# Routed experts: the activations are transposed between the next block's up products, and split first thing in a tick

## The reference

```python
# layer 0
topv, topi = jax.lax.top_k(logits, TOP_K)
gate = jax.nn.softmax(topv, -1)
weights = jnp.zeros_like(logits).at[bidx, sidx, topi].set(gate)
a = jax.nn.silu(jnp.einsum('bsd,edh->bseh', h, w1)) * jnp.einsum('bsd,edh->bseh', h, w3)
y = jnp.einsum('bseh,ehd->bsed', a, w2)
moe = jnp.einsum('bsed,bse->bsd', y, weights)
return x + moe
# layer 1
gate_up = jnp.einsum('th,eoh->teo', xf, w1)
act = _silu_and_mul(gate_up)
moe_out = jnp.einsum('te,tei,ehi->th', combine, act, w2)
return (moe_out + shared_out).reshape(B, S, Hd)
```

## Time and profile before

| | us |
|---|---|
| median of 3 runs | 2915.37 |
| lowest, highest | 2915.37, 2922.96 |
| the profiled execution | 2915.24 |
| its span (first to last instruction) | 2913.6 |
| routed experts of layer 0, in the span | about 1238 to 1605.6 |
| routed experts of layer 1, in the span | about 2486 to 2913.6 |

### The profile page before, as it was taken

How to read it: one execution, slowest core, us unless ns; L and a number is a source line. 1 busy time by engine, 2 the same in 40 slices (tenths; PEclk the granted TensorE clock), 3 DMA queues, 4 the chain that set the end, 5 groups by cost and what they waited for, 6 DMA issues and landing times. The chain is left out here.

```text
span 2913.6 us, 50292 instructions
## 1 busy us (share of the span) xinstructions
PE 2610.7 (90%) x15547; PEld 2140.7 (73%) x15548; DVE 1720.7 (59%) x3323; ACT 1130.1 (39%) x2430; POOL 782.3 (27%) x792
## 2 busy tenths in 40 slices
PE   7889879979789989879997798998999999699997
PEld 6778757768578877668875477676777788688886
DVE  4525857659676757566664447774444426566664
ACT  1102336633143324445543123564544432344442
POOL 3202200004232324423232200660000012355554
PEclk9999889999889989989998699999999989899998
DMA  4434122214532134377774432445122030666663
GB/s 158 158 115 120 26 81 71 68 38 147 145 113 61 33 121 128 117 218 226 197 215 91 119 95 47 138 135 156 56 75 71 21 114 11 189 157 159 158 159 65
DMA packets 289046, 332.99 MB, mean 114 GB/s; under 512 B 147206, under 2 KB 202454, under 8 KB 287073
## 3 DMA queue, kind: packets, MB, share of 16 engines
q1 hardware_dynamic: 216640, 250.73, 27.6%
q0 software_dynamic: 20640, 51.74, 9.2%
q10 hardware_dynamic: 51584, 28.17, 3.4%
HBM read 233.86 MB, written 96.72 MB: 113 GB/s over the span
## 5 line engine op out<-in xcount | busy, mean ns | idle before, releaser
L840 PE MATMUL e_psum<-e_up_hi,hT_hi 128*128 x672 | 245.7, 366 | 23.1 <-DVE hT_lo L810 14.6
L841 PE MATMUL e_psum<-e_up_lo,hT_hi 128*128 x672 | 237.6, 354 | 0.0
L842 PE MATMUL e_psum<-e_up_hi,hT_lo 128*128 x672 | 237.5, 353 | 0.0
L840 PEld LDWEIGHTS e_psum<-e_up_hi,hT_hi 128*128 128x128 f32 x672 | 127.4, 190 | 46.0 <-issue 33.3
L1421 POOL TENSOR_TENSOR self_a_p<-self_a_p,self_a_mx 112x448 f32<-112x448 f32 x96 | 96.6, 1007 | 228.3 <-DVE self_a_mx L1478 228.3
L816 DVE TENSOR_TENSOR hT_lo<-e_psum,hT_hi 128x256 fp32r<-128x256 f32 (+2 forms) x138 | 55.7, 435 | 154.9 <-ACT hT_hi L756 147.9
L738 ACT ACTIVATE e_gate<-e_psum 128x352 f32<-128x352 f32 (+1 forms) x86 | 44.5, 517 | 262.2 <-PE e_psum L842 261.8
L1512 ACT ACTIVATE self_a_p<-self_a_p 112x448 f32<-112x448 f32 x128 | 72.0, 575 | 179.6 <-POOL self_a_p L1421 124.5
L842 PEld LDWEIGHTS e_psum<-e_up_hi,hT_lo 128*128 128x128 f32 x672 | 127.4, 190 | 12.2
L841 PEld LDWEIGHTS e_psum<-e_up_lo,hT_hi 128*128 128x128 f32 x672 | 127.6, 190 | 10.7
L1642 PEld LDWEIGHTS joint_psum<-x_v,joint_a_pt 125*112 125x112 f32 (+1 forms) x1024 | 117.9, 176 | 21.6 <-issue 13.0
(11 more groups left out here) (550 smaller groups left out, 7384.7 us busy)
## 6 DMA issues: line engine op xcount, KB each, us to landing
e_up_raw<-in_L_ffn_w SPq DMA_DIRECT2D x64, 512.0 KB
e_up_raw<-in_L_ffn_w SPq DMA_DIRECT2D x64, 352.0 KB
e_dn_raw<-in_L_ffn_w SPq DMA_DIRECT2D x16, 1024.0 KB
q_all<-p_p_t_stage ACTq DMA_DIRECT2D x56, 256.0 KB
e_dn_raw<-in_L_ffn_w SPq DMA_DIRECT2D x16, 512.0 KB
x_q<-q_all SPq DMA_DIRECT2D x8, 896.0 KB
k_ctx<-front_c_t_stage SPq DMA_DIRECT2D x32, 187.5 KB, 2.6
v_ctx<-front_c_v_stage SPq DMA_DIRECT2D x24, 250.0 KB
```

Of the source, the lines that this page charges most:

```text
L840: pe.matmul(out, lhs[0], rhs[0], start=k == 0, stop=False)
L841: pe.matmul(out, lhs[0], rhs[1], start=False, stop=False)
L842: return pe.matmul(out, lhs[1], rhs[0], start=False, stop=k == n_k - 1)
```

## The change

Three steps move, on three engines, and one piece of code goes.

- PE: the transposes of the activations of item j-1 leave the head of the tick. They stand in the middle of the up products of item j, after two of the four blocks of the width (in the branch of an unused item, ahead of the one small product there).
- ACT: the high part of the activations is taken first thing in the next tick, and no longer at the end of its own, ahead of the split of the up weights.
- DVE: the low part is made in the next tick as well, behind the second half of the weights' split (`due_before`), and ahead of L792. It stood ahead of the one-hot table and of the first half of the split.
- The transposes behind the loop (L903 to L909) are gone: the last pair that is run no longer waits for any.

```diff
--- before.py
+++ after.py
@@ -730,6 +730,13 @@
                     act.activation(hi, raw, ACT.Copy).then_inc(dn_hi_ready, 1)
 
             def tick(j, u, item, now):
+                i = item(-1)
+                if i is not None:
+                    act.wait_ge(a_transposed, i + 1)
+                    reuse(act, y_done, i)
+                    for dst, src in a_pieces(aT[0]):
+                        last = act.activation(dst, src, ACT.Copy)
+                    last.then_inc(a_hi_ready, 1)
                 i = item(0)
                 if i is not None:
                     e, due = now.e, now.due
@@ -750,11 +757,6 @@
                     act.activation(y[:, (u - 1) % 4, :], ps[:, Y_BANK, :], ACT.Copy).then_inc(y_ready, 1)
                 i = item(0)
                 if i is not None:
-                    act.wait_ge(a_transposed, i + 1)
-                    reuse(act, y_done, i)
-                    for dst, src in a_pieces(aT[0]):
-                        last = act.activation(dst, src, ACT.Copy)
-                    last.then_inc(a_hi_ready, 1)
                     with act.If(due != 0):
                         reuse(act, y_done, i)
                         split_up(e + 1, (e + 1) % 2)
@@ -784,6 +786,12 @@
                 if item(-1) is not None:
                     with dve.If(now.due_before != 0):
                         split_up(now.e_before + 1, (now.e_before + 1) % 2, range(KC // 2, KC))
+                i = item(-1)
+                if i is not None:
+                    dve.wait_ge(a_hi_ready, i + 1)
+                    for (dst, src), (hi, _) in zip(a_pieces(aT[1]), a_pieces(aT[0])):
+                        last = dve.tensor_tensor(dst, src, hi.bitcast(F32), ALU.subtract)
+                    last.then_inc(a_ready, 1)
                 i = item(0)
                 if i is not None:
                     e, due = now.e, now.due
@@ -809,12 +817,6 @@
                     dve.wait_ge(h_hi_ready, i + 1)
                     dve.tensor_tensor(hT[1][1 - u % 2], ps[:, H_BANK, :].rearrange("p (c t) -> p c t", c=KC), hT[0][1 - u % 2].bitcast(F32),
                                       ALU.subtract).then_inc(h_ready, 1)
-                i = item(0)
-                if i is not None:
-                    dve.wait_ge(a_hi_ready, i + 1)
-                    for (dst, src), (hi, _) in zip(a_pieces(aT[1]), a_pieces(aT[0])):
-                        last = dve.tensor_tensor(dst, src, hi.bitcast(F32), ALU.subtract)
-                    last.then_inc(a_ready, 1)
                 i = item(3)
                 if i is not None:
                     coming, which = now.e_next, now.which_next
@@ -841,15 +843,17 @@
                 pe.matmul(out, lhs[0], rhs[1], start=False, stop=False)
                 return pe.matmul(out, lhs[1], rhs[0], start=False, stop=k == n_k - 1)
 
+            def turn_activations(i):
+                if i is None:
+                    return
+                pe.wait_ge(act_ready, i + 1)
+                reuse(pe, a_ready, i)
+                for c in range(n_c):
+                    last = pe.transpose(ps[0:chunks[c], A_BANK, c * 128:(c + 1) * 128], act_raw[:, offs[c]:offs[c] + chunks[c]],
+                                        core.ident[:, :])
+                last.then_inc(a_transposed, 1)
+
             def tick(j, u, item, now):
-                i = item(-1)
-                if i is not None:
-                    pe.wait_ge(act_ready, i + 1)
-                    reuse(pe, a_ready, i)
-                    for c in range(n_c):
-                        last = pe.transpose(ps[0:chunks[c], A_BANK, c * 128:(c + 1) * 128], act_raw[:, offs[c]:offs[c] + chunks[c]],
-                                            core.ident[:, :])
-                    last.then_inc(a_transposed, 1)
                 i = item(0)
                 if i is not None:
                     e, which = now.e, now.which
@@ -859,6 +863,8 @@
 
                     with pe.If(which != TT):
                         for k in range(KC):
+                            if k == KC // 2:
+                                turn_activations(item(-1))
                             pe.wait_ge(up_ready, e * KC + k + 1)
                             for part in range(2):
                                 cols = slice(part * hid, (part + 1) * hid)
@@ -899,14 +906,6 @@
                     with pe.If(which == TT):
                         pe.matmul(ps[:, Y_BANK, 0:2], aT[0][:, 0, :], aT[0][:, 0, 0:2], start=True, stop=True).then_inc(y_done, 1)
             run(pe, tick)
-
-            n_used = pe.value_load(routing.ticks[0:1, W + 5:W + 6], min_val=E, max_val=W)
-            j = n_used // 2 * 2
-            pe.wait_ge(act_ready, j + 2)
-            pe.wait_ge(a_ready, j + 1)
-            for c in range(n_c):
-                last = pe.transpose(ps[0:chunks[c], A_BANK, c * 128:(c + 1) * 128], act_raw[:, offs[c]:offs[c] + chunks[c]], core.ident[:, :])
-            last.then_inc(a_transposed, 1)
 
 
 class Segment(Stage):
```

## The result

| | before | with the change |
|---|---|---|
| median, us | 2916.55 (4 runs, 2915.37 to 2922.96) | 2962.99 (4 runs, 2957.19 to 2966.61) |
| profiled execution | 2915.24 | 2961.43 |
| its span | 2913.6 | 2959.8 |

The ratio is 1.0153 (95% interval 1.013 to 1.0176): slower by some 46 us. The forecast had the sign and the place, at 2928 us, but not a third of the size, and the measured time lies outside its range. Two executions far outside the rest, one of 14217.74 us of the kernel before and one of 8159.39 us of `e4_before_late_half`, are left out of the ratios but not out of the medians (2906.52 for that run without it).

A forecast was written before the change was run, and what follows sets the result against it. The prediction took PE, busy nearly throughout both stages, to bound the kernel. First stage +9.6 and second +3.2 gave +12.8 on the profiled 2915.24 us: forecast 2928 us, range 2912 to 2941.

The forecast's parts named there:

- the split at D+0.80: First-stage ACT: the up weights' split starts 0.79 us after the previous down products end, where today it starts 1.27 after.
- the release: Time from a late operand's end to the PE product that waited for it; taken as 0.64 us for the down products.
- due ticks: Ticks (128-token blocks of one expert) in which the next expert's up weights are split; 14 counted in each stage.
- rival A: Down products start 0.1 us behind the low part, not 0.64; some 2918 us, between 2913 and 2921; chance 0.18.
- Rival C: Transposes amid up products cost PE 0.3 in each of 84 ticks: +25, 2953 us; sign: unwaiting ticks above 9.6; chance 0.08.
- Rival B: Low pieces flow early enough that the low part isn't late and stalls go; -14.6, 2901 us; chance 0.06.
- part 4: Second-stage ticks with a split: new down-product wait of 1.0 cancels the old 0.69 `hT_lo` wait; +0.1 each, +1.4 together.
- part 3: First-stage ticks with a split: low part behind all four low pieces on DVE makes down products late; +14.4 together.
- the first kind: Eight first-stage ticks with a split, without DVE's 0.56 gap between second and third piece; 1.11 us lost each.
- Part 1: PE's moved transposes lengthen 15 second-stage ticks waiting for `hT_lo` by 0.27 each, +4.0 (or 5.5); first stage's first tick +0.4.
- Part 4, the gathers: Second-stage ticks without a split where PE waits for gathered tokens: a later tick absorbs the wait; -1.0, bounds -2 and 0.
- Part 5: Stage ends: first stage -4.0 with DVE early and POOL last, -1.2 from the earlier one-hot table; second stage -1.2.

The follow-up runs named there:

- e4_before_late_half: Kernel before, with only the second half of the up weights' low pieces moved on DVE behind `hT_lo`; 2907.55 us, ratio 0.9971.
- e3_late_half: Changed kernel with the second half of the up weights' low pieces moved on DVE behind `hT_lo`; 2916.46 us, ratio 0.9998.
- e1_pe_head: Changed kernel with PE's transposes of the activations back at the head of the tick; 2949.92 us, ratio 1.0109.
- e5_late_half_pe_head: Changed kernel with PE's transposes back at the tick's head and the second half of the low pieces behind `hT_lo`; 2908.62 us, ratio 0.9969.
- e7_onehot_tail: Kernel before with DVE's one-hot table ahead of the low part and, first stage only, the extra transposes at the end of PE's odd tick; 2905.75 us, ratio 0.9964.
- e6_onehot_first: Kernel before with one swap on DVE, the one-hot table ahead of the low part of the activations; 2911.48 us, ratio 0.9983.

## Why the forecast was too low, step by step

**Right: what is new, and where.** The wait of the down products for the low part, 14 times in each stage, the split at D+0.80 (0.79), the release of 0.68 in the tick shown (0.64 forecast; over the 28 due ticks 0.52 to 0.57 in twelve and 0.68 to 0.79 in sixteen, so rival A with 0.1 falls; this was open before), POOL last at the first stage's end. Rival C, with 0.3 in each tick, falls too: ticks of the first stage without a split took 9.54 to 9.66. Six of these sixteen are a little over the 9.6 that I had named as its sign, by 0.1 us or less against before. Rival B didn't come about, for the stream is as long as it was worked out to be.

**Wrong, first: part 4, the due ticks of the second stage.** Forecast +0.1 each, +1.4 in all; measured 14 ticks longer by 20.3 us together, 1.45 each (1.04 to 2.03; the one shown is the least). It is by far the largest miss. The step that failed is that the pieces "start about 1.2 earlier, end at 2534.5" (4.6 behind the start of the up products). In the tick shown the first piece starts 1.73 behind it, so only 0.8 earlier; in the others it starts 1.17 to 1.47 behind it, about as forecast. But then DVE stands idle between the halves, for 0.32 us in the tick shown and up to 1.04 in others, and the low part ends 5.97 behind the start in place of 5.2 (5.67 to 6.18 over the 14). The down products started 6.65 behind the up start (forecast 5.86), and the next up products 8.97 (forecast about 8.0). The old wait of 0.69 and the new one were meant to cancel; the new one came out at 1.2 to 1.6.

The view puts the idle time between the halves down to ACT. ACT's part in it had been over for long: its four pieces take 2.84 us from 2559.45, so the third was done at about 2561.6, and DVE began with it at 2562.49, 0.9 later, where it took the first up 0.2 behind its end. Between the halves DVE's sequencer reads the next item's word and takes a branch. The reading in this tick:

```profile
L562 DVEq TENSOR_LOAD <-r_ticks x1: 306/306/306, 2561.1 to 2561.1; - x1
```

In all 28 due ticks with the change the third piece began 1.05 to 1.48 us behind the end of this reading. The reading itself comes behind the sequencer's work for the second piece, and it comes at nearly the same time as before (2.1 to 2.4 us behind the up start, before 2.1 to 2.6). So the third piece began at most 0.7 earlier than before, in three ticks up to 0.16 later, however early the first one was. Before, the first two pieces were later and hid most of this: in ten of the 14 ticks there was no gap, or one of 0.04 at most. I worked this tick out by shifting the row of before, and had no gap between the halves in it. This is read from the timelines; no run changes the reading by itself. In eight of the 14 ticks the next up products stood another 0.13 to 0.89 us on "issue", 3.9 us in all, which the forecast hadn't either.

**Wrong, second: part 3, the low part's lateness in the first stage.** Forecast +14.4, measured +25.0 over the 14 due ticks. Of the eight of the first kind five took 1.57 to 2.17 more and two 1.23, where 1.11 was forecast. In the tick shown it is 0.18 for the late first piece, 0.19 for the gap between the halves, 0.04 for the release, and 0.58 more from the first down product to the next up products, 0.39 of it "issue". In three of the others the gap is 0.08 and the last term 0.12. The eighth took 3.34 more. Of the six others three took 0.88 to 0.90 (forecast 0.92), one 1.21. In those three the gap between the halves was 0.29 or 0.30, not the 0.56 I carried over from the earlier trace rows, and the release 0.52, not 0.64; that they still came out near the forecast is partly luck, since the first piece was 0.18 late. In the two worst it was 1.35 and 1.28:

```profile
1464.06 2.36 DVE L774 TENSOR_TENSOR e_up_lo<-e_up_raw,e_up_hi 128x1024 f32 x2 [1.87 <-ACT e_up_hi L725]
1467.78 2.36 DVE L774 TENSOR_TENSOR e_up_lo<-e_up_raw,e_up_hi 128x1024 f32 x2 [1.35 <-issue]
```

DVE's reading of the next item's word (L562) took 979 ns there and began when the second piece had begun, at 1465.5. Before it took 656 ns, and began ahead of the second piece:

```profile
L562 DVEq TENSOR_LOAD <-r_ticks x1: 979/979/979, 1465.5 to 1465.5; - x1
```

```profile
L562 DVEq TENSOR_LOAD <-r_ticks x1: 656/656/656, 1452.0 to 1452.0; - x1
```

The third piece began 1.3 us behind the end of the reading here too, as in all six ticks of this kind, before and with the change; so a longer or later reading comes out as a longer gap. The first two pieces, which hide part of the way, now stand 0.6 earlier. Over the six ticks the reading took 0.65 to 0.96 us before; with the change it took 0.30 in four and 0.93 and 0.98 in two. I had taken the gap as if it didn't depend on that.

**Wrong, third: the clock.** The forecast has no term for it. In the three ticks of the first stage in which it fell, the way from the first down product to the next up products took 4.44 or 4.45 us, where 2.90 to 3.01 is usual: 1.4 to 1.5 each, some 4.5 of the 25.0. What these ticks took beyond that is the longer wait itself. The views by windows gave 0.99 for both stages before, and I took this for a property of the stages; in the runs whose due ticks have no wait above 1.2 us the clock doesn't fall in any due tick past the first item's.

**The first item's due tick.** Left out as part of the filling: the tick took 11.11 for 9.57, +1.5, and 1.9 in the second stage.

**Part 1.** The tick without a split of the second stage went from 7.02 to 7.35 in the ticks bound by `hT_lo`, +0.32 to 0.34 for 0.27 with 0.1 for each change of operation beside it. All ticks without a split that grew, the first item's among them, grew by 6.8 us together (forecast 4.0; its upper bound 5.5 and the 1.9 above make 7.4). The first tick of the first stage gave +0.37 (0.4).

**Part 4, the gathers.** Forecast -1.0 with -2 as the bound, measured -8.7 over 15 ticks. Line 708 on POOL (the scattering transfer), before and then with the change, second stage:

```profile
L708 POOL DMA_INDIRECT out<-e_y,e_back x51: 1593/1597/5832, 2516.8 to 2900.9; - x51
...
  POOL e_held L707: 53.6, 26
```

```profile
L708 POOL DMA_INDIRECT out<-e_y,e_back x51: 1592/1595/2257, 2545.7 to 2947.1; - x51
...
  POOL e_held L707: 1.8, 1
```

Before, it took up to 5.83 us where DVE was in the low pieces, and 26 times the next one (L707) stood until the rows of the last had landed, 53.6 us in all. With the change the longest is 2.26. Two ticks of 9.26 and 9.17 us with a late gather became 7.45 and 7.69. That the shorter transfers gave the 8.7 is argued from these rows, and no run isolates it. Without this gain, which nobody had worked out, the change would by this sum have lost 55 us.

**Part 5.** First stage forecast -5.2, measured -3.2 (from the last up products to the stage's end, 38.2 to 35.0). POOL is last now, as said:

```profile
L81 DVEq DRAIN  x1: 17/17/17, 1617.2 to 1617.2; - x1
...
L81 POOLq DRAIN  x1: 5942/5942/5942, 1619.8 to 1619.8; - x1
```

The -1.2 for the earlier list didn't come: the wait of 2.56 for the one-hot table is gone, and one for a gather has taken its place, which the list feeds.

```profile
1604.94 1.12 PE L891 MATMUL e_psum<-ident,e_rows 128*128 128x128 f32 x4 [2.80 <-DMA e_rows<-h_rows,e_idx]
```

Second stage +0.65 for -1.2, for the same reason; its last gather wait is 2.82.

**The sum again.** First stage: due ticks 25.0, the first item's 1.5, first tick 0.4, other ticks 0.4, the way to the first up products -1.0, the end -3.2: 23.1 (forecast 9.6). Second stage: due ticks 20.3, ticks that grew 6.8, ticks that shrank -8.7, the way to the first up products 1.2, the end 0.6: 20.2 (forecast 3.2). The runs split it by cause another way. Taking the pieces out of the low part's way gives back 46 us (`e3_late_half`), of which some 9 are to be had without the change too (`e4_before_late_half`); the transposes' place costs 13 with the stream in the way (`e1_pe_head`) and 8 without (`e5_late_half_pe_head`); the shorter end gives some 4.6 back (`e7_onehot_tail` against `e6_onehot_first`). They add up only roughly, since each wait that goes lets another one show.

**Open.** Why the clock fell behind a wait of 1.58 us in one tick and not behind others as long, and in `e1_pe_head` behind one of 1.54 and not behind one of 2.33. Why the reading of the item's word took 0.93 and 0.98 us in two ticks, and 0.30 in the others. What the 0.13 to 0.89 us of "issue" ahead of the up products in the second stage are; in `e3_late_half` waits of the same lengths are put down to `e_up_lo`. What of the first stage's 5.2 us in `e5_late_half_pe_head` is the place of the transposes.

## To carry to other kernels

When a step moves behind a stream of operations that another engine feeds, work out the stream's pace with each hand-over, with a gap at every boundary of the program in it, and with the sequencer's work that can no longer run ahead; the 28 due ticks took 45.3 us more where 15.8 were forecast, about one microsecond more in each. Work each stage out from its own rows; a wait that you let cancel against another needs both their ends on one time line. What stands ahead of a long stream on the same engine is the cheap thing to swap: one operation moved into an idle stretch, and one wait at the end freed, made the kernel before faster by 0.36% (`e7_onehot_tail`).

## What the runs showed of the hardware that I had not expected

- TensorE's granted clock fell to 1.2 GHz for about 3 us behind single waits of 1.54 to 2.35 us, in stages whose middle has 0.99 before: products 0.42 us apart for 0.23, about 1.5 us lost each time. Other waits of the same lengths, up to 2.33, left it alone.
- POOL's descriptor work for one scattering transfer (L708) took 1.6 us or up to 5.8 us, depending on what DVE did at the time. The Trainium skill, GPSIMD Engine Reference, section Specifications, says that POOL shares its SBUF interfaces with VectorE and contends with DVE instructions that have two SBUF inputs; the low pieces (L772: raw and high part, both in SBUF) are such instructions. The rows agree in part. In the second stage before, the nine transfers that took 4.09 us or more each lay over 3.2 to 3.5 us of low pieces; but with the change seven lay over 1.17 us of them and took 1.59 as without. No run here isolates it.
- A product that was released by a late operand, with a branch and the addresses behind the wait, started 0.64 to 0.78 us behind it at the up products, and 0.52 to 0.57 or 0.68 to 0.79 at the down products.
- With the change, DVE's third piece started 1.05 to 1.48 us behind the end of its sequencer's reading of a word from SBUF (0.30 to 0.98 us), though the data it needed had been ready for 0.6 us or more.
